# A routed feed-forward layer on one core: chunks of 128 tokens and one of 103 in place of five chunks of 123

## What is computed

```
probs = softmax(layernorm(x) @ Wr + br);  gates, ids = top_k(probs, 2)
# per expert: the 615 tokens with the largest gates -> disp_tok, disp_g
xg  = x[disp_tok].reshape(8, 615, 512)
h   = silu(einsum('ecd,edh->ech', xg, W1) + b1)        # hidden size 2048
out = einsum('ech,ehd->ecd', h, W2) + b2
y   = zeros(4096, 512).at[disp_tok].add(out * disp_g)
x   = x + tanh(g_ffn) * y
```

## Time and profile before

| | |
|---|---|
| median of 3 runs | 1873.83 us (1872.61 to 1874.28) |
| the profiled execution's own time | 1872.92 us |
| its span in the profile | 1871.2 us |
| granted TensorE clock, mean | 0.972 |
| TensorE busy | 1760.9 us, 94% |
| DVE, ACT, POOL busy | 59%, 42%, 24% |
| HBM read and written | 134.08 MB and 43.63 MB |

### The profile page before, as it was taken

The page is one execution under the profiler, slowest core; times in us unless marked ns, Lnnn a source line. Parts: engine busy times, 40 slices in busy tenths (PEclk is TensorE's granted clock), DMA queues, the critical chain, the costliest instruction groups (busy, mean ns, idle before and its releaser), DMA issues.

```text
span 1871.2 us, 29771 instructions
## 1 busy us (share of the span) xinstructions
PE 1760.9 (94%) x10546; PEld 907.9 (49%) x10546; DVE 1110.0 (59%) x2143; ACT 778.9 (42%) x1013; POOL 452.9 (24%) x424
## 2 busy tenths in 40 slices
PE   7999999999999999999922999999999999999996
PEld 4334243342423324233211767666666767666664
DVE  6777777778777787777577544526262534434331
ACT  4453635446354453534540624334251615344330
POOL 2322424123242233321211112112212122112102
PEclk9999999999999999999955999999999999999998
DMA  6313233132321404214032362626355363627301
GB/s 221 101 45 114 69 107 118 45 112 68 129 96 65 133 27 134 90 42 139 7 130 77 93 159 65 175 71 168 77 135 128 98 158 84 172 50 190 78 26 25
DMA packets 175167, 188.16 MB, mean 101 GB/s; under 512 B 82452, under 2 KB 123552, under 8 KB 171016
## 3 DMA queue, kind: packets, MB, share of 16 engines
q1 hardware_dynamic: 134152, 167.03, 28.6%
q0 software_dynamic: 40960, 20.41, 6.3%
HBM read 134.08 MB, written 43.63 MB: 95 GB/s over the span
## 4 chain that ended last, share of the span: by engine, by line
PE 82%; DVE 9%; issue 3%; ACT 2%; DMA 2%; POOL 1%; SPq 0%; DVEq 0%; ACTq 0%; POOLq 0%
PE psum L1529 22%; PE psum L1506 20%; PE psum L1328 7%; PE psum L1335 7%; PE psum L1319 6%; PE psum L1309 6%; PE psum L1299 5%; PE psum L1421 4%; PE psum L1346 2%; DVE mx L909 2%; PE psum L1228 2%; ACT osum L773 1%; DVE reached L1053 1%; DVE x2hl L973 1%; DVE x2hl L975 1%
## 5 line engine op out<-in xcount | busy, mean ns | idle before, releaser
L1529 PE MATMUL psum<-w,hT 128*123 128x512 f16 x1920 | 415.7, 379 | 0.0
L1506 PE MATMUL psum<-xgT,w 128*128 128x369 f16 (+1 forms) x3072 | 409.8, 295 | 0.9 <-DVE xgT L1154 0.8
L909 DVE TENSOR_REDUCE mx<-psum 128x1 f32<-128x512 f32 x512 | 331.1, 683 | 107.9 <-PE psum L1309 105.8
L1506 PEld LDWEIGHTS psum<-xgT,w 128*128 128x128 f16 x3072 | 297.8, 97 | 109.2 <-DVE xgT L1154 1.0
L1529 PEld LDWEIGHTS psum<-w,hT 128*123 128x123 f16 x1920 | 260.5, 136 | 152.8
L762 ACT ACTIVATE pt<-psum 128x1024 f32<-128x1024 f32 x256 | 259.1, 1021 | 166.4 <-PE psum L1319 165.8
L832 ACT ACTIVATE h<-psum,b1c 128x369 f32<-128x369 f32 (+1 forms) x256 | 117.8, 511 | 326.3 <-PE psum L1506 325.8
L1175 DVE TENSOR_TENSOR hT<-h,hT 128x615 f16<-128x615 f32 x128 | 102.5, 801 | 211.5 <-ACT hT L835 211.5
L665 POOL DMA_INDIRECT out_dram<-y,idx_now x40 | 99.6, 2490 | 481.8 <-DVE y L1207 253.3
L1204 DVE SCALAR_TENSOR_TENSOR y<-psum,b2b 123x512 f32<-123x512 f32 x40 | 27.7, 691 | 268.0 <-PE psum L1529 268.0
L1299 PE MATMUL psum<-actT,wT 128*128 128x512 f16 x768 | 179.2, 381 | 2.0 <-DVE wT L896 2.0
(11 more groups left out here) (184 smaller groups left out, 1549.5 us busy)
## 6 DMA issues: line engine op xcount, KB each, us to landing
stage<-in_L_ffn_W_dram SPq DMA_DIRECT2D x62, 1024.0 KB, 6.2
stk<-qk_rows SPq DMA_DIRECT2D x192, 128.0 KB, 2.5
qk_rows<-qks SPq DMA_DIRECT2D x64, 256.0 KB, 2.5
xin<-in_x_dram SPq DMA_DIRECT2D x8, 1024.0 KB, 5.4
cin<-in_ctx_dram SPq DMA_DIRECT2D x8, 1024.0 KB, 7.6
xres<-in_x_dram SPq DMA_DIRECT2D x8, 1024.0 KB, 5.7
out_dram<-xres SPq DMA_DIRECT2D x32, 256.0 KB, 2.1
x_split<-x2hl SPq DMA_DIRECT2D x32, 256.0 KB, 2.3
```

The costliest lines, as they stand in the source:

```text
L909: v.reduce_max(mx[:, KT * t + qt:KT * t + qt + 1], ps, AX.X).then_inc(read, 1)
L1506: mm = t_.matmul(psum[:, (2 * m + ch) % 4, 0:(c1 - c0) * CP], w1[:, wp, kt, m * P:(m + 1) * P], xgT[:, c0:c1, KT * xp + kt, 0:CP], start=( ...
L1529: mm = t_.matmul(psum[0:CP, Y_BANK[c], :], hT[:, hp, k, c * CP:(c + 1) * CP], w2[:, wp, k, :], start=(k == 0 and (hp, wp) == (0, 0)), stop ...
```

## The change

The chunk size becomes 128 rows; the last chunk has the 103 that are left of 615. Everything that had 123 rows or columns has 128 (`hot`, `iota_p`, `by_tile`, the tables of indices and gates, the gathers), and the gather of the last chunk fetches 128 rows too, its last 25 with index 0. `xgT` is laid out by depth piece first, so that all 615 tokens of a piece lie side by side, and a pair of first products takes 308 and 307 of them. The second products, DVE's two operations and the scatters take the chunks in the order 4, 0, 1, 2, 3, and chunk 4 has 103 rows there. The clearing of `xg` is gone. The core of the diff:

```diff
-C = 5
-CP = CAP // C
-assert C * CP == CAP and CP <= P
+C = -(-CAP // P)
+CHUNK_ORDER = (C - 1,) + tuple(range(C - 1))
...
+def chunk_rows(c):
+
+    return min(P, CAP - c * P)
...
-        xgT = sb("xgT", [P, C, 2 * KT, P], f16)
+        xgT = sb("xgT", [P, 2 * KT, C * P], f16)
...
-        CHUNKS = ((0, 3), (3, C))
+        CHUNKS = ((0, 308), (308, CAP))
...
-                    sp.dma_start(xgT[:, c, :, :], xg[:, c, :], transpose=True).then_inc(xgT_in, 16)
+                    sp.dma_start(xgT[:, :, c * P:(c + 1) * P], xg[:, c, :], transpose=True).then_inc(xgT_in, 16)
...
-                if isinstance(n, int) and n == 0:
-                    pool.wait_ge(xg_cleared, 1)
-                elif isinstance(n, int) and n == 1:
+                if isinstance(n, int) and n == 1:
                     pool.wait_ge(xgT_full, C)
...
-                        out=xg[0:CP, c, :], out_offset=None, in_=x2_split[:, :],
+                        out=xg[:, c, :], out_offset=None, in_=x2_split[:, :],
...
-                for c in range(C):
-
-
-                    pool.wait_ge(y_ready, C * e + c + 1)
-                    if c == 0:
+                for i, c in enumerate(CHUNK_ORDER):
+                    rows = chunk_rows(c)
+
+                    pool.wait_ge(y_ready, C * e + i + 1)
+                    if i == 0:
                         pool.wait_ge(y_added, 16 * C * e)
                     settle(pool)
                     g.indirect_dma_start(
-                        out=out_rows, out_offset=bass.IndirectOffsetOnAxis(ap=idx_now[:, c:c + 1], axis=0),
-                        in_=y[:, c, :], in_offset=None, compute_op=ALU.add).then_inc(y_added, 16)
+                        out=out_rows, out_offset=bass.IndirectOffsetOnAxis(ap=idx_now[0:rows, c:c + 1], axis=0),
+                        in_=y[0:rows, c, :], in_offset=None, compute_op=ALU.add).then_inc(y_added, 16)
...
-            s.activation(xg[96:P, :, :].rearrange("p c d -> p (c d)"), ident[96:P, 0:1].to_broadcast((P - 96, C * 2 * D)),
-                         ACT.Copy, scale=0.0).then_inc(xg_cleared, 1)
...
-                                mm = t_.matmul(psum[:, (2 * m + ch) % 4, 0:(c1 - c0) * CP], w1[:, wp, kt, m * P:(m + 1) * P],
-                                               xgT[:, c0:c1, KT * xp + kt, 0:CP], start=(kt == 0 and (wp, xp) == (0, 0)),
+                                mm = t_.matmul(psum[:, (2 * m + ch) % 4, 0:c1 - c0], w1[:, wp, kt, m * P:(m + 1) * P],
+                                               xgT[:, KT * xp + kt, c0:c1], start=(kt == 0 and (wp, xp) == (0, 0)),
...
-                            mm = t_.matmul(psum[0:CP, Y_BANK[c], :], hT[:, hp, k, c * CP:(c + 1) * CP], w2[:, wp, k, :],
+                            mm = t_.matmul(psum[0:rows, Y_BANK[i], :], hT[:, hp, k, c * P:c * P + rows], w2[:, wp, k, :],
```

More of the change, by code:

```diff
@@ L178, in layer_kernel @@
         ident16 = sb("ident16", [P, P], f16)
-        hot = sb("hot", [P, NT, CP], bf16)
-        iota_p = sb("iota_p", [P, CP], bf16)
+        hot = sb("hot", [P, NT, P], bf16)
+        iota_p = sb("iota_p", [P, P], bf16)
         slot_p = sb("slot_p", [P, E, NT], f32)
@@ L401, in bank16_rows @@
         def bank16_rows(k):
-            even = CP + CP % 2
-            return psum[:, k, :].bitcast(f16)[:, 0:2 * KT * even].rearrange("p (i q) -> p i q", q=even)[:, :, 0:CP]
+            return psum[:, k, :].bitcast(f16).rearrange("p (i q) -> p i q", q=P)
         @block.sync
@@ L639, in gather @@
                 pool.wait_ge(tab_read, 2 * n + 2)
-                if isinstance(n, int) and n == 0:
-                    pool.wait_ge(xg_cleared, 1)
-                elif isinstance(n, int) and n == 1:
+                if isinstance(n, int) and n == 1:
                     pool.wait_ge(xgT_full, C)
-                else:
+                elif not isinstance(n, int):
                     pool.wait_ge(xgT_in, 16 * C * n - 16 * C)
@@ L1195, in expert @@
                 dve.wait_ge(idx_kept, 2 * e + 2)
-                for c in range(C):
-                    if more >= 1:
-                        if c < 4:
-                            for q in range(4):
-                                split_quarter(8 * e + 8 + c, c, q, 1)
-                    dve.wait_ge(y_full, C * e + c + 1)
-                    dve.wait_ge(y_ready, C * e + c)
-                    v.scalar_tensor_tensor(y32[:, :], psum[0:CP, Y_BANK[c], :], 1.0 / SW, b2b[:, :],
+                for i, c in enumerate(CHUNK_ORDER):
+                    rows = chunk_rows(c)
+                    if more >= 1 and i < 4:
+                        for q in range(4):
+                            split_quarter(8 * e + 8 + i, i, q, 1)
+                    dve.wait_ge(y_full, C * e + i + 1)
+                    dve.wait_ge(y_ready, C * e + i)
+                    v.scalar_tensor_tensor(y32[0:rows, :], psum[0:rows, Y_BANK[i], :], 1.0 / SW, b2b[0:rows, :],
                                            ALU.mult, ALU.add).then_inc(y_biased, 1)
-                    dve.wait_ge(y_biased, C * e + c + 1)
-                    v.tensor_scalar(y[:, c, :], y32[:, :], gate_now[:, c:c + 1], None, ALU.mult).then_inc(y_ready, 1)
+                    dve.wait_ge(y_biased, C * e + i + 1)
+                    v.tensor_scalar(y[0:rows, c, :], y32[0:rows, :], gate_now[0:rows, c:c + 1], None, ALU.mult).then_inc(y_ready, 1)
             expert(0, 2)
@@ L1467, in table @@
                         pe.wait_ge(hot_ready, NT * n + t + 4)
-                    mm = t_.matmul(psum[32 * j:32 * j + 32, 5, 0:CP], val_e[:, t, :], hot[:, t, :],
+                    mm = t_.matmul(psum[32 * j:32 * j + 32, 5, 0:P], val_e[:, t, :], hot[:, t, :],
                                    start=(t < 4), stop=(t >= NT - 4))
@@ L1474, in select_slots @@
                 pe.wait_ge(tab_copied, n + 1)
-                t_.matmul(psum[0:CP, 5, 256:256 + 2 * C], by_tile[:, :], select[:, :], start=True, stop=True).then_inc(tab_full, 1)
+                t_.matmul(psum[:, 5, 256:256 + 2 * C], by_tile[:, :], select[:, :], start=True, stop=True).then_inc(tab_full, 1)
             table(0)
@@ L1484, in _ @@
                 for i in range(2 * KT):
-                    last = t_.transpose(bank16_rows(6 + c % 2)[:, i, :], xg[0:CP, c, i * P:(i + 1) * P], ident16[0:CP, 0:CP])
+                    last = t_.transpose(bank16_rows(6 + c % 2)[:, i, :], xg[:, c, i * P:(i + 1) * P], ident16[:, :])
                 last.then_inc(xgT_full, 1)
@@ L1514, in expert @@
                         select_slots(e + 1)
-                for c in range(C):
-                    if c == 0:
+                for i, c in enumerate(CHUNK_ORDER):
+                    rows = chunk_rows(c)
+                    if i == 0:
                         pe.wait_ge(y_biased, C * e)
-                    elif c == 1:
+                    elif i == 1:
                         if not last:
@@ L1522, in expert @@
                     else:
[L1523 removed]
+                        pe.wait_ge(y_biased, C * e + i - 1)
                     for k in range(MT):
[L1525 removed]
+                        if i == 0:
                             pe.wait_ge(h_ready, MT * e + k + 1)
```

38 lines of the change are left out of this document (18 added, 20 removed).

## The result

| | before | after |
|---|---|---|
| median | 1874.19 us (1872.61 to 1874.94, 5 runs) | 1864.09 us (1861.77 to 1864.84, 5 runs) |
| the profiled execution, its span | 1872.92, 1871.2 us | 1861.77, 1860.1 us |
| mean granted clock | 0.972 | 0.976 |

The ratio is 0.9944, with a 95% interval of 0.9932 to 0.9955: the change makes the kernel 10.1 us faster. Forecast was 1861.6 us, and 1855 to 1868.

A forecast was written before the change was run, and what follows sets the result against it. TensorE, busy 94% of the span, was taken as the bound, with a hole before and a tail behind its matmuls. Terms -5.8 - 4.3 - 2.6 + 0.5 = -12.2 us gave 1861.6 us, range 1855 to 1868.

The forecast's parts named there:

- The tail: Behind the last matmul: the last scatter's 128 rows use 16 engines, not three; 2.5 us in place of 8.3, -5.8 us.
- The hole: Before the first expert's first product: gathers over 16 engines, the last landing in 4.6 us, not 8.9; -4.3 us.
- The first products: In the experts' long stretch: one piece per matmul removes 4/5 of a 2.1 ns excess a pair; -2.6 us.
- the bound of nothing: Limit on the first products' gain: zero if the excess belongs to the weight load or something the change keeps.
- The wait for the table copy: Before the slot selection: TensorE's seven waits for DVE's copy of the table grow 0.07 us each, +0.5 us.
- POOL's own time: At both ends: POOL's 2.40 us for a scatter and 1.43 us for a gather were kept unchanged.
- rival 3: In tail and front: POOL's time falls with the descriptors, 3.5 us more gain, 1858.1 us; chance 25%.
- The short chunk: Each expert's first scatter: 103 rows on one engine take about 21 us, covered by the work before anything needs them.
- rival 4: Between experts: the one-engine scatter holds up the stage loads of the next w1, slower, 1889.6 us; chance 3%.
- the sentence on DVE's indices: Nothing needs the scatters until DVE overwrites the indices at m = 4 of the next expert, 12.6 us into its products.
- Nothing from the weight loads: Second products: weight loads of 128 columns take 97 ns, not 136, but lie beside the preceding matmul; no gain taken.

The follow-up runs named there:

- the later version: The changed kernel with first-product pairs of 312 + 304 columns and the first expert's w2 loads held until its fifth gather landed: 1857.86 us, ratio 0.9915.

## Why the prediction was right, and where not

**The tail** (-5.8 forecast, -6.04 measured). The mechanism, three engines for 123 rows and sixteen for 128, is shown by 112 and 113 rows in the kernel before. The packets took the 2.5 us of the forecast, but not by its two parts, 1.5 us at 10.4 GB/s an engine and 1.0 of a slow start: there was no slow start, and the sixteen engines moved 106 GB/s, 6.6 each. Two terms were missing, POOL's -0.84 and +0.6 behind the last packet, and nearly cancelled. So the sum is closer than the working deserved.

**The hole** (-4.3 forecast, -4.43 measured): right in its sum and wrong in its parts. The landing was to fall from 8.9 to 4.6 us and fell to 6.6; the crowding by the stage loads was named and taken as a doubling of 1.2 us, and measures 2.8 us. POOL, taken as unchanged, issued the last gather 2.1 us sooner (its five gathers took it 6.42 us and not 8.39). Two errors of 2 us cancelled, which is luck. 1019.91 is just ahead of the 1020 to 1021 that were to be seen, since DVE's first quarter came 0.71 us sooner.

**The first products** (-2.6 forecast, 0.0 measured): this step failed. I took the excess of 2.1 ns a pair as one column's time for each odd piece, and with one piece in each matmul it stayed. The excess is real, but it hangs on the column counts: 369 + 246 and 308 + 307 both pay about 2 ns a pair, 312 + 304 none. One measured pair had been taken for its cause, where the bound of nothing already named another, "something the change keeps". That the later version gained just these 2.6 us doesn't make the step right.

**The wait for the table copy** (+0.5 forecast, none measured). The seven waits are 1.9 us and were 2.0. ACT's second bank did take the 0.05 us longer (308 and 307 columns at 512 ns in the mean, 458 before); but the path from the 23 products ahead of the selection to the 216 behind it is 3.94 us before and 3.96 after, so 0.02 us a wait and not 0.07.

**POOL's own time** (rival 3, 25%, 3.5 us more) came in direction: 0.84 us in the tail and 2.1 in front, 2.9 together. It was not a rival beside the forecast but a part of it, and what it gave was lost again in the landing of the last gather and behind the last packet.

**The short chunk** (rival 4, and the sentence on DVE's indices): its cover held with the short chunk first, since TensorE and DVE wait no more than before, although its rows are on the way for long: in the second expert it is issued at 1190.17, and between 1216 and 1222 us a row still goes about every 0.26 us. What the lead is worth, the run with the short chunk last shows: without the four chunks behind it the kernel loses 65 us against the change, of which the tail is 17. The prediction named the wait and its cover, but priced no rival on it.

**Nothing from the weight loads** was right: PEld's busy time fell from 907.9 to 845.2 us and the second products stayed at 51.81 us.

The total fell short by 1.1 us in the profiled execution (-12.2 forecast, -11.1 measured) and by 2.5 in the median. The stretch of the experts was to be 2.1 us shorter (2.6 less 0.5) and is 0.1 longer, so 2.2 are missing; 0.2 and 0.1 more came from tail and hole, and 0.7 from the earlier first quarter, which differs by more than that between two profiles of one kernel. So the number is right partly by luck: one of three terms was not there, and the two that were had wrong parts that cancelled.

## What to carry to other kernels

Look at the row count of every indirect DMA whose end somebody waits for: 112 or 128 rows go over sixteen engines here, 123 over three, 113 and 103 over one. In the middle of the kernel a slow one costs nothing as long as the work between its issue and whoever needs it is longer than its landing: here 16.8 us covered a landing of 12 us, and not one of 24. When a stage is shortened at its edges, look at what is issued next to the transfer that ends it; two 1 MB loads issued 0.65 us behind a gather cost 2.8 us. Then ask what the next limit is; here it was DVE, and it was reached. In a dense stream of matmuls try a multiple of 8 moving columns, padding one if need be, and measure such a price with a sweep inside one kernel before giving it a cause.

## What the hardware showed that I had not expected

- A matmul over 308 or 307 columns, or 309 and 307, takes longer than its columns: pairs of 263.3 to 266.7 ns, against 261.5 to 261.7 ns for the ten splits of 616 into multiples of 8 that were tried, down to 512 + 104.
- POOL's time for the kernel's last scatter goes with the rows that it gives to one engine: 1.49 us for 7, 1.56 for 8, 2.40 for 41, 4.06 for 103, 4.35 for 113, about 0.026 us a row.
- POOL's queue has half of the packets after the change, 21120 for 40960, with 20.67 and 20.41 MB. A scatter on fewer engines has more packets, not fewer: 144 for 128 rows, 672 for 123, 1664 for 103, the surplus being 8 bytes each.
- A scatter of 103 accumulated rows of 2 KB on one engine lands 24 us after its issue, and TensorE, having stood for 5.0 to 6.4 us, works at a granted clock of 0.50 for about 3 us behind it.
